# Moving a stack's load behind the shift rows on the SP queue, and splitting the wait ahead of them

## Chip, core and metric

The kernel runs on one core of one Trainium2 chip. The metric is the device time of one execution in microseconds. Engines are named as in the profile: PE (TensorE matmul), PEld (its weight loads), DVE (VectorE), ACT (ScalarE), POOL (GpSimd) and SP (SyncE, which computes nothing here and issues nearly all DMAs).

## What is computed

One transformer layer in float32 on x of shape 2 x 1024 x 512: `x = x + attn(layernorm(x))`, then `x = x + ffn(layernorm(x))`. The diff touches the attention:

```python
qkv = clip(einsum('bsd,ed->bse', x, Wqkv), -8, 8); q, k, v = split(qkv)
q = layer_norm(q, q_ln_w, q_ln_b); k = layer_norm(k, k_ln_w, k_ln_b)   # then 32 heads of 16
scores = einsum('bqhd,bkhd->bhqk', q, k) * 0.25 + slope[h] * (key - query)
probs = softmax(where(key <= query, scores, -1e30))
out = einsum('bsd,ed->bse', einsum('bhqk,bkhd->bqhd', probs, v), Wout)
```

The feed-forward part is a 512 x 512 matrix that is summed from four sign matrices with their row factors.

## The kernel before, in words

**Three stages.** First 16 tiles of 128 rows are normalised, projected, and q and k are split into three bf16 parts each (high, middle, low), turned and stored to DRAM in `parts_dram`; v goes to `v_dram`. Then 16 groups of heads (GROUPS; a group is 4 heads of one of the two sequences) go through the attention. Last, 16 output tiles take the output projection and the feed-forward part.

**A group.** Its scores are products of bf16 stacks. The *first* stack (`first_q`, `first_k`) has the three leading products of parts and six bias rows, the *second* (`second_q`, `second_k`) the three smaller products, rows for the causal steps, and two rows with the *shift*: the negative of each query's maximum over its keys, as a high and a low bf16 part. Each is held in a ring of three buffers (STACKS = 3). For each group PE first makes the scores of the first stack alone (`score_max`, L1078), and DVE takes their maxima (`take_max`, L951). DVE joins them (L921), PE turns them (L1147), ACT negates them and writes `shift` and `shift_hi` (L764, L765; each counts up `shift_hi_ready`), and POOL makes `shift_lo` (L653, which counts up `shift_ready`). SP copies the four rows (high and low, for two halves of the partitions) into `second_q` (`load_shift`, L476), each row 4 KB. Only then can the group's own scores be made with both stacks (`score`, L1098), which ACT exponentiates (L781) and PE multiplies by v (`weigh`, L1133). After each half of the queries ACT copies the sums out (`copy_half`, L809) and SP stores them.

**The order on PE, DVE, ACT and POOL** is written out by steps: a group has 40 of them (NE = 40 entries), and step s of each engine's `exp_step` does entry s of the exponentials and, beside it, one piece of the maxima of a later group. With EARLY = 14, the maxima of group k+2 begin at step 26 of group k, and the maxima of group k+1 are turned at step 28 of group k (TURN_AT = 28), so 12 steps are left until group k+1 begins at step 40. At a group's first step PE waits for `second_loaded` and `shift_loaded` (L1092, L1093). Before the first piece of the maxima it waits for `first_loaded` (L1066).

**The order on SP** is the order of `group_step(s)`, one call per group, and SP works through it strictly in turn: a wait on SP holds back everything behind it. Before: for group s+2, wait until group s-1's scores are done (L495), `load_first` (16 DMAs: twelve of 64 KB from `parts_dram`, L428, and four bias rows, L436) and `load_second` (14 DMAs: twelve of 64 KB and two bias rows; for groups 0 to 2 also four with step rows, L449); then `load_values(s+1)` (L468, 512 KB), behind a wait for the last product with v of group s-1; then the stores of the second half of group s-1 and the first half of group s (L506, 256 KB each), behind the waits for their copies; then `load_shift(s+1)`, behind its wait (L472). Groups 0 and 1 have their stacks loaded during the projections, and `load_shift(0)` stands ahead of the first call of `group_step`.

Of the kernel before, what the change touches and what calls it, by code (L numbers as in the profile page):

```python
# [24 lines left out]
GROUPS = BATCH * HEADS // G  # L25
# [152 lines left out]
def build(nc, x, wqkv_t, qk_w, qk_b, wout_t, bases_t, alphas, bias_rows, step_rows, masks, out):  # L178
# [7 lines left out]
    def sem(name):  # L186
        return ctx.enter_context(nc.semaphore(name))
# [8 lines left out]
    with ctx:  # L196
# [121 lines left out]
        shift_hi_ready, shift_ready = sem("shift_hi_ready"), sem("shift_ready")  # L318
# [54 lines left out]
        def _(sp):  # L373
# [48 lines left out]
            def load_terms(n, i, dst, terms, loaded):  # L422

                for half in range(PAIR):
                    for r, term in enumerate(terms):
                        at = half * HALF_ROWS + r * HD
                        slot = term[0] if i == 0 else 5 - term[1]
                        sp.dma_start(dst[at:at + HD, :, :],  # L428
                                     parts_dram[slot, n // GPB, n % GPB * HD:(n % GPB + 1) * HD, half]
                                     ).then_inc(loaded, 16)  # L430

            def load_bias(n, i, dst, row, last, loaded):

                for half in range(PAIR):
                    at = half * HALF_ROWS + NT * HD
                    sp.dma_start(dst[at:at + last - row, :, :], bias_rows[i, n % GPB, half, row:last]).then_inc(loaded, 16)  # L436

            def load_first(n):
                for i, dst in ((0, first_q[n % STACKS]), (1, first_k[n % STACKS])):
                    load_terms(n, i, dst, TERMS[:NT], first_loaded[n % STACKS])  # L440
                    load_bias(n, i, dst, 0, BIAS_ROWS, first_loaded[n % STACKS])

            def load_second(n):
                loaded = second_loaded[n % STACKS]
                for i, dst in ((0, second_q[n % STACKS]), (1, second_k[n % STACKS])):
                    if n < STACKS:
                        for half in range(PAIR):
                            at = half * HALF_ROWS + SECOND_K
                            sp.dma_start(dst[at:at + STEP_ROWS, :, :], step_rows[i]).then_inc(loaded, 16)  # L449
                    load_terms(n, i, dst, TERMS[NT:], loaded)  # L450
                load_bias(n, 1, second_k[n % STACKS], BIAS_ROWS, BIAS_ROWS + SHIFT_ROWS, loaded)
# [15 lines left out]
            def load_values(n):  # L467
                sp.dma_start(v_sb[n % 2][:], v_dram.rearrange("b g k p n -> (b g) k p n")[n]  # L468
                             .rearrange("k p n -> p k n")).then_inc(v_loaded[n % 2], 16)

            def load_shift(n):
                sp.wait_ge(shift_ready, n + 1)  # L472
                for r, part in ((0, shift_hi), (1, shift_lo)):
                    for half in range(PAIR):
                        row = half * HALF_ROWS + NT * HD + r
                        sp.dma_start(second_q[n % STACKS][row:row + 1, :, :].rearrange("p a t -> p (a t)"),  # L476
                                     part[n % 2][half * PAIR * TPB:(half + 1) * PAIR * TPB, :]
                                     ).then_inc(shift_loaded[n % 2], 16)
# [6 lines left out]
            projections_over()  # L485
            load_last_weights()
            load_shift(0)
            parts_over()

            def group_step(s):  # L490

                n = s + 2
                if 2 <= n < GROUPS:
                    if n >= STACKS:
                        sp.wait_ge(scored, NE * (n - STACKS + 1))  # L495
                    load_first(n)
                    load_second(n)

                n = s + 1
                if 2 <= n < GROUPS:  # L500
                    sp.wait_ge(pv_done, NU * (n - 1))
                    load_values(n)
                for n, half in ((s - 1, 1), (s, 0)):
                    if 0 <= n < GROUPS:
                        sp.wait_ge(o_ready, 2 * n + half + 1)
                        sp.dma_start(o_dram[n // GPB, :, ds((n % GPB) * G, G), half * BANK:(half + 1) * BANK]  # L506
                                     .rearrange("r j t -> j r t"), o_sb[half][:]).then_inc(o_stored[half], 16)

                n = s + 1
                if 1 <= n < GROUPS:  # L510
                    load_shift(n)

                if s == GROUPS - 2:
                    load_sums(0)
                if s == GROUPS - 1:
                    store_inverses(0)

                    sp.wait_ge(inv_stored, 16)
                    sp.wait_ge(wout_ready, DC)
                    sp.wait_ge(wffn_ready, DC)  # L520
                    for t in range(3):
                        if t == 2:
                            sp.wait_ge(att_ready, 1)
                        load_sums_of_tile(t)
                        load_residual(t)

            def load_sums_of_tile(t):

                sp.dma_start(o_in[t % 2][:], o_dram[t // TPB, 0:HD, :, ds((t % TPB) * P, P)]
                             .rearrange("(c r) h t -> (r h) c t", c=DC)).then_inc(o_loaded[t % 2], 16)  # L530
                rows = inv_dram[t // TPB, :, ds((t % TPB) * P, P)]
                sp.dma_start(inv_in[t % 2][:], rows.rearrange("(a h) t -> a h t", a=1)
                             .broadcast_to([HD // DC, HEADS, P])).then_inc(o_loaded[t % 2], 16)

            def load_residual(t):
                sp.dma_start(x2[t % 4][:], x[t]).then_inc(xr_loaded[t % 4], 16)

            def load_sums(b):

                for half in range(2):  # L540
                    sp.wait_ge(o_stored[half], 16 * (GROUPS if b else GROUPS - 1 - half))
                sp.dma_start(sums[:, b, :], o_dram[b, HD].rearrange("h (q t) -> (h q) t", q=P // HEADS)
                             ).then_inc(sums_loaded, 16)

            def store_inverses(b):
                sp.wait_ge(inverted, b + 1)
                sp.dma_start(inv_dram[b].rearrange("h (q t) -> (h q) t", q=P // HEADS),
                             inv[:, b, :]).then_inc(inv_stored, 16)

            run_groups(sp, group_step)  # L550

            def output_step(s):
# [722 lines left out]
```

## Time and profile before

| | us |
|---|---|
| median of 3 runs | 721.72 |
| lowest and highest of them | 720.21 and 725.4 |
| the profiled execution's own time | 724.78 |
| its span, first to last instruction | 723.0 |

The span is what the rows below are taken from; 1.8 us of the profiled execution lie outside it. Times of rows are microseconds from the start of the span. A "releaser" is what ended the idle time before an instruction, as inferred from semaphores; "issue" means that the profile shows no releaser. SPq is SP's queue of DMA issues: the duration there is what SP spent on issuing, not the transfer. "To landing" is from the issue to the last byte.

### The profile page before, as it was taken

To read this page: it belongs to the slowest core of one execution; us is meant where nothing else is said; L and a number is where in the kernel's file an instruction comes from. 1 tells how busy PE (TensorE), PEld (TensorE's weight loads), DVE (VectorE), ACT (ScalarE), POOL (GpSimd) and SP (SyncE) were. 2 spreads that over 40 slices of the span, in tenths; PEclk is the share of its full clock that TensorE was granted. 3 is DMA by queue.
4 is the path that set the end of the run, shared out by engine and by line. 5 is a ranking of instruction groups with operands and counts; after the bars stand their busy time and mean duration, and the time that the engine had idled before them with its cause. 6 is when DMAs were issued, how large, how long until landed. Compare 5 with 4: busy or idle time off the path is not lost.

```text
span 723.0 us, 16007 instructions
## 1 busy us (share of the span) xinstructions
PE 678.8 (94%) x6096; PEld 416.4 (58%) x6096; DVE 575.2 (80%) x990; ACT 411.4 (57%) x855; POOL 312.9 (43%) x403
## 2 busy tenths in 40 slices
PE   3999999997999999999999999999899896599998
PEld 2888888883354454444455455444445532488886
DVE  6799999988999889998998899799899810275664
ACT  5132333232078778887787788678778886222221
POOL 1377777777034625525426422322332234444440
PEclk9999999997579999999999999999999999699999
DMA  8225556777884342343344334324434111635441
GB/s 297 65 68 174 175 175 194 199 201 215 264 183 106 117 127 86 98 125 116 90 123 122 91 108 125 110 78 125 114 94 117 50 35 23 170 103 156 145 148 66
DMA packets 102060, 93.64 MB, mean 130 GB/s; under 512 B 11640, under 2 KB 81912, under 8 KB 101984
## 3 DMA queue, kind: packets, MB, share of 16 engines
q1 hardware_dynamic: 97856, 86.84, 41.4%
q10 hardware_dynamic: 2016, 3.67, 1.7%
q0 software_dynamic: 2112, 2.10, 1.5%
q8 instruction: 49, 0.80, 0.5%
q14 instruction: 27, 0.22, 0.1%
HBM read 57.44 MB, written 33.82 MB: 126 GB/s over the span
## 4 chain that ended last, share of the span: by engine, by line
PE 71%; DVE 15%; issue 8%; POOL 3%; ACT 2%; DMA 1%; SPq 0%; DVEq 0%; POOLq 0%; ACTq 0%
PE ps L1098 23%; PE ps L1133 20%; PE ps L1078 9%; PE ps L1012 5%; PE ps L1013 5%; PE ps L1014 5%; DVE stats L951 3%; DVE qk_stat L896 2%; DVE qk L892 2%; PE ps L1020 2%; PE ps L1074 2%; DVE x_stat L862 1%; DVE xt_lo L855 1%; DVE rest L871 1%; DVE v_ext L905 1%
## 5 line engine op out<-in xcount | busy, mean ns | idle before, releaser
L951 DVE TENSOR_REDUCE stats<-ps 128x1 f32<-128x512 f32 (+3 forms) x608 | 359.4, 656 | 43.9 <-PE ps L1078 42.2
L781 ACT ACTIVATE probs<-ps 128x512 f32<-128x512 f32 (+2 forms) x640 | 310.2, 560 | 83.4 <-PE ps L1098 82.9
L1078 PE MATMUL ps<-first_k,first_q 54*128 54x128 bf16 (+3 forms) x1152 | 219.9, 284 | 5.6 <-DVE stats L951 5.2
L1098 PE MATMUL ps<-second_q,second_k 64*128 64x128 bf16 (+4 forms) x1152 | 206.2, 276 | 0.0
L1098 PE MATMUL ps<-first_q,first_k 54*128 54x512 bf16 (+3 forms) x768 | 197.0, 331 | 9.3 <-issue 9.2
L673 POOL TENSOR_SCALAR_AFFINE_SELECT probs<-probs 128x256 f32<-128x256 f32 x256 | 102.5, 406 | 144.2 <-ACT probs L781 136.9
L1133 PE MATMUL ps<-probs,v_sb 128*32 128x512 f32 (+3 forms) x1536 | 157.9, 498 | 1.8 <-issue 0.8
L1098 PEld LDWEIGHTS ps<-first_q,first_k 54*128 54x128 bf16 x768 | 58.2, 95 | 121.8 <-ACT probs L781 108.1
L1078 PEld LDWEIGHTS ps<-first_k,first_q 54*128 54x128 bf16 x1152 | 92.7, 96 | 49.3 <-DVE stats L951 34.7
L1098 PEld LDWEIGHTS ps<-second_q,second_k 50*128 50x128 bf16 (+1 forms) x1152 | 92.9, 96 | 21.4 <-issue 2.1
L1012 PE MATMUL ps<-wqkv_hi,xt_hi 128*128 128x512 f32 x192 | 77.3, 403 | 0.0
L1014 PE MATMUL ps<-wqkv_hi,xt_lo 128*128 128x512 f32 x192 | 75.8, 395 | 0.0
L1013 PE MATMUL ps<-wqkv_lo,xt_hi 128*128 128x512 f32 x192 | 75.7, 394 | 0.0
L614 POOL TENSOR_TENSOR qk<-qk,qk_gain 128x1024 f32<-128x1024 f32 x16 | 38.4, 2399 | 59.9 <-DVE qk L913 59.9
L653 POOL TENSOR_TENSOR shift_lo<-shift,shift_hi 32x128 bf16<-32x128 f32 x16 | 6.7, 418 | 131.8 <-ACT shift_hi L765 131.8
L973 DVE TENSOR_TENSOR x<-ps,x 128x512 f32<-128x512 f32 x16 | 11.0, 687 | 58.9 <-PE ps L1014 58.9
L1133 PEld LDWEIGHTS ps<-probs,v_sb 128*32 128x32 f32 x1536 | 33.9, 108 | 34.9 <-ACT probs L781 15.1
L1074 PE MATMUL ps<-mask_sb 64*128 64x256 bf16 x256 | 51.0, 280 | 0.0
L751 ACT ACTIVATE qk_sd<-qk_mv,eps 128x2 f32<-128x2 f32 x16 | 4.7, 296 | 69.6 <-DVE qk_mv L899 69.6
L1014 PEld LDWEIGHTS ps<-wqkv_hi,xt_lo 128*128 128x128 f32 x192 | 36.6, 191 | 8.0
L1012 PEld LDWEIGHTS ps<-wqkv_hi,xt_hi 128*128 128x128 f32 x192 | 36.8, 191 | 7.2
L1013 PEld LDWEIGHTS ps<-wqkv_lo,xt_hi 128*128 128x128 f32 x192 | 36.7, 191 | 7.2
(79 smaller groups left out, 822.1 us busy)
## 6 DMA issues: line engine op xcount, KB each, us to landing
parts_dram<-parts SPq DMA_DIRECT2D x48, 256.0 KB, 4.0
v_dram<-v_ext SPq DMA_DIRECT2D x16, 512.0 KB, 4.0
v_sb<-v_dram SPq DMA_DIRECT2D x16, 512.0 KB, 4.4
o_dram<-o_sb SPq DMA_DIRECT2D x32, 256.0 KB
first_q<-parts_dram SPq DMA_DIRECT2D x96, 64.0 KB
first_k<-parts_dram SPq DMA_DIRECT2D x96, 64.0 KB
second_q<-parts_dram SPq DMA_DIRECT2D x96, 64.0 KB
second_k<-parts_dram SPq DMA_DIRECT2D x96, 64.0 KB
```

The lines of the kernel that those rows point to most:

```text
L614: pool.tensor_tensor(qk[t % 2][:], qk[t % 2][:], qk_gain[:], ALU.mult).then_inc(qk_scaled, 1)
L673: pool.affine_select(out=turned, in_=turned, compare_op=ALU.is_ge, fill=0.0, base=0, pattern=[[0, 2], [1, P]], channel_multiplier=-1).then ...
L781: act.activation(weights, scores, ACT.Exp, scale=SCALE).then_inc(exp_done, 1)
L892: dve.tensor_scalar(qk[t % 2][:], ps[:, bank:bank + 2, :], CLIP, -CLIP, ALU.min, ALU.max).then_inc(qk_clipped, 1)
L951: dve.tensor_reduce(to, scores, AX.X, ALU.max).then_inc(max_taken, 1)
L1012: pe.matmul(to, hi[:, c, :], w_hi[:, c, :], start=(c == 0), stop=False)
L1013: pe.matmul(to, hi[:, c, :], w_lo[:, c, :], start=False, stop=False)
L1014: last = pe.matmul(to, lo[:, c, :], w_hi[:, c, :], start=False, stop=(c == DC - 1))
L1074: pe.matmul(ps[:, bank, :].rearrange("p (r h t) -> p r h t", r=G, h=2)[:, :, h, :], late_q[h][mine, :], one_hot[mine, :, :], start=(h == 0 ...
L1078: last = pe.matmul(ps[:, bank, r * cols:(r + 1) * cols], first_q[n % STACKS][rows, hp, i * P:(i + 1) * P], first_k[n % STACKS][rows, hp, k ...
L1098: return pe.matmul(ps[:, bank, r * cols + first:r * cols + last], stack_k[n % STACKS][rows, heads[r] // PAIR, kb * P:(kb + 1) * P], stack_ ...
L1133: last = pe.matmul(ps[j * VW:(j + 1) * VW, PV_BANK, to:to + cols], v_sb[n % 2][:, kb, j * VW:(j + 1) * VW], probs[w % P_SLOTS][:, j, 0:col ...
```

## The change

In `load_shift(n)` SP issues the two high rows after `shift_hi_ready` has reached 2(n+1), which both copies of ACT give, and waits for `shift_ready` only ahead of the two low rows. In `group_step` `load_second(s+2)` no longer stands behind `load_first(s+2)`, but behind `load_shift(s+1)`.

```diff
             def load_shift(n):
-                sp.wait_ge(shift_ready, n + 1)
                 for r, part in ((0, shift_hi), (1, shift_lo)):
+                    if r == 0:
+                        sp.wait_ge(shift_hi_ready, 2 * (n + 1))
+                    else:
+                        sp.wait_ge(shift_ready, n + 1)
                     for half in range(PAIR):
                         row = half * HALF_ROWS + NT * HD + r
                         sp.dma_start(second_q[n % STACKS][row:row + 1, :, :].rearrange("p a t -> p (a t)"),
...
                     if n >= STACKS:
                         sp.wait_ge(scored, NE * (n - STACKS + 1))
                     load_first(n)
-                    load_second(n)
...
                 n = s + 1
                 if 1 <= n < GROUPS:
                     load_shift(n)
+
+                n = s + 2
+                if 2 <= n < GROUPS:
+                    load_second(n)
```

## Rows read from the trace of the kernel before

**Rows 1.** The page's busy times: us (share of the span) xinstructions

```profile
PE 678.8 (94%) x6096; PEld 416.4 (58%) x6096; DVE 575.2 (80%) x990; ACT 411.4 (57%) x855; POOL 312.9 (43%) x403
```

**Rows 2.** Waits, PE's: us in total, times, longest us

```profile
PE ps L1098 <- issue: 9.2, 7, 1.9
...
PE ps L1133 <- ACT o_sb L809: 0.7, 2, 0.4
```

**Rows 3.** Timeline of PE, short stretches: start us, us, instruction [idle before <-releaser]

```profile
243.31 0.28 PE L1147 MATMUL ps<-ident,peak 128*32 128x128 f32 x1
...
296.21 0.28 PE L1147 MATMUL ps<-ident,peak 128*32 128x128 f32 x1
...
321.03 0.28 PE L1147 MATMUL ps<-ident,peak 128*32 128x128 f32 x1
...
330.35 0.37 PE L1098 MATMUL ps<-first_q,first_k 54*128 54x512 bf16 x1 [1.69 <-issue]
...
347.72 0.28 PE L1147 MATMUL ps<-ident,peak 128*32 128x128 f32 x1
...
579.94 0.27 PE L1147 MATMUL ps<-ident,peak 128*32 128x128 f32 x1
```

**Rows 4.** Timeline of SP's queue, groups 4 and 5

```profile
319.84 1.19 SPq L506 DMA_DIRECT2D o_dram<-o_sb  x2
322.83 2.23 SPq L476 DMA_DIRECT2D second_q<-shift_hi  x2
325.10 1.23 SPq L476 DMA_DIRECT2D second_q<-shift_lo  x2
328.69 2.64 SPq L428 DMA_DIRECT2D first_q<-parts_dram  x6
...
342.44 1.19 SPq L506 DMA_DIRECT2D o_dram<-o_sb  x2
349.51 1.20 SPq L476 DMA_DIRECT2D second_q<-shift_hi  x2
```

**Rows 5.** Tile shift_lo's transfers, windows 322:331, 349:354 and 195:200.6 in turn

```profile
DMA to landing us min/median/max: 4.0/4.3/4.5
...
DMA to landing us min/median/max: 2.1/2.2/2.2
...
DMA to landing us min/median/max: 1.8/1.8/1.8
```

**Rows 6.** Waits of SP's DMA queue: us in total, times, longest us

```profile
SPq L476 <- POOL shift_lo L653: 66.9, 16, 6.9
...
SPq L428 <- PE ps L1098: 40.4, 13, 3.7
```

**Rows 7.** Windows: us, PE, PEld, DVE, ACT, POOL busy, PEclk, DMA share, GB/s

```profile
252.00:257.00 5.00, 4.34 (x36) 1.97 (x40) 3.06 (x5) 2.59 (x5) 0.77 (x3) 0.69 0.38 112
...
252.70:278.70 26.00, 25.89 (x304) 12.96 (x306) 22.26 (x38) 19.87 (x42) 7.16 (x16) 0.93 0.36 104
...
457.70:483.80 26.10, 25.97 (x303) 12.98 (x304) 22.25 (x38) 19.86 (x42) 5.91 (x15) 0.93 0.35 102
```

**Rows 8.** Timeline of SP's queue at the start of the attention

```profile
198.88 2.84 SPq L428 DMA_DIRECT2D first_q<-parts_dram  x6
...
205.84 0.74 SPq L449 DMA_DIRECT2D second_q<-in_step_rows  x2
...
214.08 0.58 SPq L436 DMA_DIRECT2D second_k<-in_bias_rows  x2
```

**Rows 9.** Timeline of ACT and of POOL at the turn in group 4

```profile
322.05 0.26 ACT L765 ACTIVATE shift_hi<-ps 32x128 bf16<-32x128 f32 x1
...
322.38 0.42 POOL L653 TENSOR_TENSOR shift_lo<-shift,shift_hi 32x128 bf16<-32x128 f32 x1 [9.37 <-ACT shift_hi L765]
```

**Rows 10.** Timeline of ACT and of DVE in group 5

```profile
342.23 0.59 ACT L809 ACTIVATE o_sb<-ps 128x512 f32<-128x512 f32 x1
...
347.18 0.25 DVE L921 TENSOR_REDUCE peak<-stats 128x32 f32<-128x96 f32 x1
```

## The prediction

> **What bounds the kernel now.** I read the page's busy times first, then the waits, then the timeline around them. PE is busy for 678.8 us, 94% of the span, and no other engine comes over 80% [rows 1], so only PE's idle time can be won, and what a stall costs it beside that. The change touches SP alone, in the attention. There the waits of PE are few: seven times it stood ahead of a product of L1098 with no releaser shown, 9.2 us in all and up to 1.9 [rows 2]. One of the seven is the row at 330.35, idle 1.69 us before it [rows 3], and it is the first product of group 5. Two semaphores are waited for there, the second stack's and the shift rows'. The stack was issued a whole group earlier. The shift rows were not: SP issued the two low ones from 325.10 for 1.23 us [rows 4], the last of them thus at about 325.7, and the longest landing of the two is 4.5 us [rows 5], which gives 330.2. So the shift rows end this wait. SP itself has time: it waits 66.9 us for shift_lo in 16 waits, and 40.4 us for PE at the head of a group's step [rows 6].
>
> What the stalls cost can be read without adding up gaps. Every group turns its maxima at the same step. From 296.21 to 321.03 no stall lies between, and the distance is 24.82 us; from 321.03 to 347.72, across the stall at 330.35, it is 26.69 [rows 3]. So this stall of 1.69 costs 1.87, as PE has to fill its buffers again. From the turn at 243.31 to the one at 579.94 there are 13 groups in 336.63 us, where 13 x 24.82 are 322.66: 14.0 us too many [rows 3]. They hold all seven stalls, and something else too: two groups, from 252.70 and from 457.70, took 26.0 and 26.1 us without a stall at their end, and the mean granted clock in both is 0.93; in the first of them it is 0.69 from 252.0 to 257.0 [rows 7], so the lower of the two levels (1.2 instead of 2.4 GHz) was granted early in the group. Against 24.82 this cost 1.2 and 1.3 us. Both groups began with a stall; yet that at 330.35 brought no dip, as its 26.69 is 24.82 and the 1.87 above. So 14.0 is about 9.2 of idle time, 2.5 of clock, 1.3 of refilling (seven times 0.18) and 0.7 of waits for o_sb in the last groups [rows 2], which the change leaves, with 0.3 over.
>
> **Why the rows land late.** Three cases stand in [rows 4, 5]. Ahead of group 5 the stores of o_sb are issued until 321.03 and the high rows from 322.83, 1.8 us later: the low rows take 4.0 to 4.5 us to land. Ahead of group 6 the stores end at 343.63, the high rows start at 349.51, 5.9 us later: 2.1 to 2.2 us. At the start of the attention, with nothing before them for a long time and a load issued right behind them (198.88) [rows 8], they take 1.8 us. So what is issued shortly before the rows holds them up, and what is issued behind them does not. What stands before them is a burst: 30 loads of stacks in about 13 us, 512 KB of v, and two stores of 256 KB.
>
> **The change, part by part.** *The split wait.* Now the high rows wait for POOL's shift_lo, which takes 0.42 us and ends at 322.80; ACT's copy ends at 322.31 [rows 9]. After it the high rows start 0.5 us sooner. A pair takes about 1.2 us to issue [rows 4], more than those 0.5, so the low rows find their wait over and also go 0.5 us sooner, not 1.2. The wait added on shift_hi_ready costs nothing: what stands behind it on SP stood behind a later wait before. Alone this part is worth 0.5 us of each stall.
>
> *The moved load.* Take group 5 (starts 330.35) as the pattern, times from its start. Before, first and second stack go out in one run, then v, then the stores until +13.3 (343.63), and the high rows at +19.2. After, only the first stack is issued early in the step, six terms in 2.64 us [rows 4] and two bias rows in 0.58 [rows 8], both twice, with small gaps: 6.6 us. The store of the first half must wait for its copy, which ends at 342.82 [rows 10], +12.5; the store, one of 0.6 us, is out at +13.1. The v load and the other store, which had stood right before it, go 3 us earlier, at about +10. The high rows start at +18.6, 5.5 us behind a store of 256 KB that is alone, nearly what gave 2.1 to 2.2 us. In a group like 4, where the old run ended 1.8 us ahead of the rows, 6 us of issuing are gone from before them. So the last low row is issued at 18.6 + 1.9 = +20.5 and lands at +22.7. The next group starts at +24.7. This leaves 2.0 us, more than one long issue costs (1.0: two high rows took 2.23 in one case and 1.20 in the other) [rows 4]. Value: the stalls vanish, and with them the clock's two dips, 14.0 - 0.7 = 13.3 us. Bounds: 14.0 if all goes; from below 7 x 0.5 = 3.5 if the landings stay as late as they are.
>
> *The second stack, where it goes now.* Its 14 issues start at +21.1 and take two times 2.64 and 0.58 [rows 4, 8] with small gaps, 6.0 us, until +27.1; it is needed a group and a half later, so it costs nothing itself. But SP's queue is past the next group's start (+24.7) by 2.4 us, and by 3.4 with one long issue. The wait at L428, which hid behind 40.4 us of idling, gets shorter and pays for it. The first stack of the next step is then issued from +2.4 to +9.0. PE wants it where DVE joins the maxima before, 347.18 [rows 10], +16.8. So 7.8 us are left for landing and long issues; the longest landing of a row shown is 4.5 us. Costed at nothing, in all groups but one. In group 1 the stack moved behind the rows is group 2's, with step rows: at the start of the attention it took from 205.84 to 214.66, 8.8 us [rows 8]. Group 1 starts at about 243.31 - 17.37 = 225.9 (its turn, less what lies from start to turn in group 5) [rows 3]. By the pattern the moved stack goes out 3.6 us before that, at 222.3, and ends at 231.1; the first stack ends at 237.7, or 238.7 with one long issue, and is wanted at 225.9 + 16.8 = 242.7. That leaves 4.0 to 5.0 us for a landing which for the rows was 1.8 to 4.5 and may be longer for a load behind 18 others (6 us as my upper estimate, the 4.5 and a third more): a wait of 0 to 2.0. I take 0.7, and 0.3 for shift rows that this makes late once, 1.0 in all.
>
> **The sum.** 724.8 - 13.3 + 1.0 = 712.5 for an execution like the profiled one. The median is 3.1 us lower, and the three runs spread over 5.2 us. Stalls and dips are what can differ from run to run, as the long issues and the dips come where they like; a kernel without them should be steadier, but part of the 3.1 may lie elsewhere. I take off half: 711.0, 10.7 us or 1.5% below the median. A measurement here can tell about 1% from no change.
>
> The Trainium skill (DMA: Bandwidth & Descriptors, section "Anatomy of one DMA — SWDGE (gpsimd) path") fits a DMA as about 2.0 us fixed plus its bytes over the bandwidth, given for POOL's path. For a row of 4 KB that is 2.0 us whatever stands before it. By it the last row ahead of group 5 would have landed at 327.7, and the stall would be another's. Those landings [rows 5] agree with it for the quiet cases (1.8 and 2.2) and not for 4.0 to 4.5. The case in which it holds is the third rival.
>
> **Rivals.**
> 1. *The rows stay late.* If the one store ahead of them holds them up as two stores and a v load did, only the 0.5 us come off: 7 x 0.5 = 3.5, so 721.72 - 3.5 = 718.2. For it: the store writes to DRAM and is the last thing before the rows in both orders. Against it: 5.9 us after two of them nothing was left.
> 2. *The clock dips anyway.* PE stands idle no more, yet the two dips stay: 711.0 + 2.5 = 713.5. For it: a stall of 1.69 us had none, so the stall alone doesn't decide. Against it: both came early in a group that a stall had opened.
> 3. *Not the load.* The rows land late for a cause that isn't in SP's order, and the 0.5 us is eaten by it: 721.7, no change.
> 4. *The first stack becomes late, slower.* Place: PE's wait for first_loaded in each group from 1 to 12. It decides from the point where the first stack takes over 7.8 us from its last issue to landing, as it now queues behind 14 loads issued right before it, and no longer into an empty queue. At 9.1 us it costs 1.3 us in each of 12 groups, 15.6, and keeps the dips (2.5): 711.0 + 18.1 = 729, which is slower than before. For it: a backlog of 30 loads plainly is there now, as it holds the rows up. Against it: these rows still land within 4.5 us with a v load and two stores on top.
>
> **Chances.** Forecast 0.62, rival 1 0.15, rival 2 0.12, rival 3 0.06, rival 4 0.05. The forecast's own range is from 707.7 (724.8 - 14.0 and the whole 3.1 off) to 714. The range given reaches to rival 1: 707.0 to 718.5. Faster by over 1% (below 714.5) is the forecast and most of rival 2: 0.72. Within 1%: rivals 1 and 3 and the rest, 0.24. Slower by over 1%: 0.04.
>
> **What would show it.** Right: the row "L1098 <- issue" of PE's waits falls from 9.2 us in seven to under 2; shift_lo's landings have a longest of under 3 us; SP's order shows second_q behind shift_lo; turn to turn is 24.8 us in nearly all groups and their clock 1.00. The wait of SP at L428 falls well below 40.4 us. Wrong: PE's waits at L1098 stay near half of what they were (rival 1), or a new wait of PE ahead of L1078 with no releaser shows, near 16.8 us into a group (rival 4), or groups without a stall keep a clock of 0.93 (rival 2).

## The result, and the profile after

| | before, us | after, us |
|---|---|---|
| median (6 runs each) | 724.71 | 711.43 |
| lowest and highest | 720.21 to 727.1 | 709.58 to 712.45 |
| the profiled execution | 724.78 | 710.61 |
| its span | 723.0 | 708.9 |

The ratio on record is 0.983, 95% interval 0.980 to 0.986: 1.7% faster (the two medians alone give 0.982). The forecast was 711.0 in a range of 707.0 to 718.5, so the time is right. The gain against these six runs, 13.3 us, is more than the 10.7 forecast from three of them; on the chips of the experiments the kernel before has medians of 720.67 to 722.53, and in run 10 the changed kernel is 11.8 us ahead of it. The runs also lie closer together, 2.9 us apart against 6.9. The changed kernel's lines have moved: L1098 of before is L1104, L1078 is L1084, L1147 is L1153, L951 is L957, the stores' L506 is L508 and the rows' L476 is L479.

The page of the changed kernel has for all products of the scores with the first stack, those at the groups' starts among them (busy us, mean ns | idle us before them):

```profile
L1104 PE MATMUL ps<-first_q,first_k 54*128 54x512 bf16 (+3 forms) x768 | 193.8, 328 | 0.1
```

The idle time before them is 0.1 us, where the waits had 9.2 in seven [rows 2]. The turns in PE's timeline, as in [rows 3]:

```profile
241.91 0.28 PE L1153 MATMUL ps<-ident,peak 128*32 128x128 f32 x1
...
316.35 0.28 PE L1153 MATMUL ps<-ident,peak 128*32 128x128 f32 x1
...
341.17 0.28 PE L1153 MATMUL ps<-ident,peak 128*32 128x128 f32 x1
...
565.26 0.27 PE L1153 MATMUL ps<-ident,peak 128*32 128x128 f32 x1
```

From 316.35 to 341.17 are 24.82 us, and from 241.91 to 565.26, the same 13 groups, 323.35. That is 0.7 us over 13 x 24.82, where it was 14.0. Of the span's 14.2 us, 13.3 are gained here; 1.4 more were gained ahead of the first of these turns (nearly all of it in the projections, where the two kernels don't differ) and 0.5 lost behind the last. The windows of two groups, columns as in [rows 7], show a granted clock of 1.00 where it was 0.93:

```profile
249.30:274.10 24.80, 24.80 (x311) 12.39 (x308) 22.66 (x39) 20.25 (x44) 8.08 (x19) 1.00 0.37 109
447.80:472.60 24.80, 24.80 (x311) 12.39 (x308) 22.67 (x39) 20.25 (x44) 6.84 (x18) 1.00 0.42 116
```

SP's timeline around group 5, which starts at 323.71, answers to [rows 4]:

```profile
326.78 0.58 SPq L436 DMA_DIRECT2D second_k<-in_bias_rows  x2
327.40 2.62 SPq L428 DMA_DIRECT2D first_q<-parts_dram  x6
...
334.28 0.67 SPq L436 DMA_DIRECT2D first_k<-in_bias_rows  x2
335.00 0.39 SPq L468 DMA_DIRECT2D v_sb<-v_dram  x1
335.43 1.42 SPq L508 DMA_DIRECT2D o_dram<-o_sb  x2
342.46 1.20 SPq L479 DMA_DIRECT2D second_q<-shift_hi  x2
343.71 1.21 SPq L479 DMA_DIRECT2D second_q<-shift_lo  x2
```

The lines show that the moved stack ends at 327.36, inside the next group, and the first stack at 334.95, +11.2. The stores end at 336.85, +13.1, and the rows follow 5.6 us later. (Where the text says that a store ends, its issue is meant; it lands later.) All low rows of the kernel, before and after in turn:

```profile
DMA to landing us min/median/max: 1.7/2.5/5.0
```

```profile
DMA to landing us min/median/max: 1.7/1.8/3.5
```

The longest landing of after, 3.5 us, is ahead of group 12 and cost nothing, as 0.67 us were left. Its row was issued 7.5 us behind the stores, and those had landed before; what held it isn't known.

What SP pays is in its waits; the second row was 40.4 us [rows 6]:

```profile
SPq L508 <- ACT o_sb L815: 37.4, 16, 8.3
...
SPq L428 <- PE ps L1104: 0.7, 3, 0.3
```

### The profile page after: what moved, and what is told of

Its sections match the earlier page's. It is cut to its first block, busy times and chain, and to the rows that moved or that the text cites. A ratio compares the mean times of both kernels' runs of the same rounds, so it can differ in the third digit from the quotient of the medians.

```text
span 708.9 us, 16007 instructions
## 1 busy us (share of the span) xinstructions
PE 674.5 (95%) x6096; PEld 413.3 (58%) x6096; DVE 575.5 (81%) x990; ACT 410.3 (58%) x855; POOL 313.2 (44%) x403
## 4 chain that ended last, share of the span: by engine, by line
PE 73%; DVE 15%; issue 7%; POOL 2%; DMA 2%; ACT 1%; SPq 0%; DVEq 0%; POOLq 0%; ACTq 0%
PE ps L1104 23%; PE ps L1139 20%; PE ps L1084 9%; PE ps L1018 6%; PE ps L1020 5%; PE ps L1019 5%; DVE stats L957 4%; PE ps L1026 2%; DVE qk_stat L902 2%; DVE qk L898 2%; PE ps L1080 2%; DVE x_stat L868 1%; DVE xt_lo L861 1%; DVE rest L877 1%; DVE v_ext L911 1%
## 5 line engine op out<-in xcount | busy, mean ns | idle before, releaser
L957 DVE TENSOR_REDUCE stats<-ps 128x1 f32<-128x512 f32 (+3 forms) x608 | 358.3, 656 | 31.6 <-PE ps L1084 29.3
L1084 PE MATMUL ps<-first_k,first_q 54*128 54x128 bf16 (+3 forms) x1152 | 217.3, 282 | 5.1 <-DVE stats L957 4.5
L1104 PE MATMUL ps<-second_q,second_k 64*128 64x128 bf16 (+4 forms) x1152 | 204.6, 273 | 0.0
L1104 PE MATMUL ps<-first_q,first_k 54*128 54x512 bf16 (+3 forms) x768 | 193.8, 328 | 0.1
L1104 PEld LDWEIGHTS ps<-first_q,first_k 54*128 54x128 bf16 x768 | 57.6, 94 | 110.5 <-ACT probs L787 107.6
L1084 PEld LDWEIGHTS ps<-first_k,first_q 54*128 54x128 bf16 x1152 | 92.3, 96 | 51.0 <-DVE stats L957 36.0
L1104 PEld LDWEIGHTS ps<-second_q,second_k 50*128 50x128 bf16 (+1 forms) x1152 | 91.7, 95 | 21.0 <-issue 0.6
```

Source lines behind the costliest of these rows:

```text
L957: dve.tensor_reduce(to, scores, AX.X, ALU.max).then_inc(max_taken, 1)
L1084: last = pe.matmul(ps[:, bank, r * cols:(r + 1) * cols], first_q[n % STACKS][rows, hp, i * P:(i + 1) * P], first_k[n % STACKS][rows, hp, k ...
L1104: return pe.matmul(ps[:, bank, r * cols + first:r * cols + last], stack_k[n % STACKS][rows, heads[r] // PAIR, kb * P:(kb + 1) * P], stack_ ...
```

## The experiments

All times are medians. Ratios are against the kernel before on the same chip, with their 95% interval.

**1. The split wait alone.** The kernel before, with only this:

```diff
             def load_shift(n):
-                sp.wait_ge(shift_ready, n + 1)
                 for r, part in ((0, shift_hi), (1, shift_lo)):
+                    if r == 0:
+                        sp.wait_ge(shift_hi_ready, 2 * (n + 1))
+                    else:
+                        sp.wait_ge(shift_ready, n + 1)
```

> The kernel before with the split wait alone; the load stays where it was. Theory (the rows land late because of the loads and stores issued shortly before them; the split gives only the 0.5 us by which ACT's copy is earlier than POOL's): stalls stay at 5 to 7 groups, each shorter by up to 0.5 us, so 2 to 4 us faster than before (before: 724.7 median of six), with 0 to 2 dips of the clock left; the low rows' landings still reach 4 to 5 us. Rival (the split carries the gain, since the low rows leave 1.2 us sooner): stalls nearly gone, 9 us faster or more, about 713.

Measured: 722.70, ratio 1.0017 (0.9985 to 1.0049): nothing, at most 0.2% of gain. The waits of PE in its profile, SP's stores and the high rows ahead of group 5, their low rows' landings, and the stall:

```profile
PE ps L1101 <- issue: 6.8, 6, 2.3
```

```profile
317.25 1.19 SPq L509 DMA_DIRECT2D o_dram<-o_sb  x2
320.01 1.52 SPq L479 DMA_DIRECT2D second_q<-shift_hi  x2
```

```profile
DMA to landing us min/median/max: 4.3/4.6/4.8
```

```profile
327.62 0.37 PE L1101 MATMUL ps<-first_q,first_k 54*128 54x512 bf16 x1 [1.28 <-issue]
```

The stores ended at 318.44, and PE could go on at 327.62, 9.2 us later. Before, the stores ended at 321.03 and PE went on at 330.35 [rows 3, 4], 9.3 us later. The high rows left 1.3 us behind the turn's start at 318.71 instead of 1.8, and the low ones took longer to land, 4.3 to 4.8 us against 4.0 to 4.5 [rows 5]. So it isn't their issue that sets when they land, but when the stores went out. Both theories fall: the split gives neither 9 us nor 0.5 us a stall.

**2. The moved load alone.** The changed kernel with the old wait:

```diff
                 for r, part in ((0, shift_hi), (1, shift_lo)):
-                    if r == 0:
-                        sp.wait_ge(shift_hi_ready, 2 * (n + 1))
-                    else:
-                        sp.wait_ge(shift_ready, n + 1)
```

(and `sp.wait_ge(shift_ready, n + 1)` ahead of the loop again).

> The changed kernel with the old single wait on shift_ready; the load stands behind the rows. Theory: in the changed kernel the last row landed 0.67 us or more before each group's first product, 2.4 us in the typical group, so 0.5 us later rows still arrive in time: no stall or one of 0.1, turns 24.8 us apart, the time within 0.3% of the changed kernel's 711.4, landings 1.8 to 3.5 us. Rival (the split is needed too): stalls in several groups, 714 or more.

Measured: 711.29, ratio 0.9861 (0.9828 to 0.9894), turns 24.8 us apart in the profiled execution, from the second to the fifteenth. One of the six runs took 715.53, the others 708.81 to 711.89; it wasn't profiled, so stalls can't be ruled out there. The theory holds: the move is all of the gain that can be measured, and the split shows none in either order.

**3. The second stack right ahead of the rows.** The changed kernel with these two in the other order:

```diff
+                n = s + 2
+                if 2 <= n < GROUPS:
+                    load_second(n)
+
                 n = s + 1
                 if 1 <= n < GROUPS:
                     load_shift(n)
-
-                n = s + 2
-                if 2 <= n < GROUPS:
-                    load_second(n)
```

> The changed kernel, but the second stack goes out after the stores and right ahead of the rows' wait, so it is out of the first stack's run and yet ahead of the rows: 14 loads from +13.1 to +19.1 of a group, the rows from +19.2. Theory (what is issued shortly before the rows holds them up): a stall in every group, landings of 3 to 5 us, 1 to 2.5 us each, 15 to 35 us slower than the changed kernel, so slower than before. Rival A (only the stores to DRAM hold the rows up, loads into the chip's memory don't): rows land in about 2 us, no more than 0.6 us late in issue, no stalls, about 711 to 714. Rival B (it is the length of the run of 30 loads that matters): no stalls either.

Measured: 713.48, ratio 0.9892 (0.9861 to 0.9923). SP's timeline ahead of the rows for group 6, those low rows' landings, and PE's waits:

```profile
339.32 3.32 SPq L428 DMA_DIRECT2D second_q<-parts_dram  x6
342.69 3.98 SPq L428 DMA_DIRECT2D second_k<-parts_dram  x6
346.71 0.57 SPq L436 DMA_DIRECT2D second_k<-in_bias_rows  x2
347.32 1.20 SPq L479 DMA_DIRECT2D second_q<-shift_hi  x2
```

```profile
DMA to landing us min/median/max: 1.8/1.8/1.8
```

```profile
PE ps L1104 <- issue: 0.9, 1, 0.9
```

My theory expected a stall in every group here. With 14 loads issued up to the last 0.04 us before them, the rows land in 1.8 us, as fast as anywhere. The rows were issued late instead (3.7 us behind the turn at 343.58, where 1.3 is usual), which cost one stall, in group 1. The last low rows ahead of groups 1 to 15 took 1.8 us in 12 cases; the others are 2.1, 2.6 and 3.3 us, with the stores issued 8 us and more before. So 14 such loads hold the rows up little or not at all.

**4. The store behind the rows.** The kernel before, the second stack in its old place, with

```diff
-                for n, half in ((s - 1, 1), (s, 0)):
+                for n, half in ((s - 1, 1),):
...
                     load_shift(n)
+                for n, half in ((s, 0),):
+                    if 0 <= n < GROUPS:
+                        sp.wait_ge(o_ready, 2 * n + half + 1)
+                        sp.dma_start(o_dram[...], o_sb[half][:]).then_inc(o_stored[half], 16)
```

> The kernel before with the store of the first half's sums moved behind the rows; the load stays. Ahead of the rows stand then the 30 loads, v and one store that is issued 0.6 us sooner. Theory (the whole backlog counts, of which this store is one of 32 transfers): stalls shrink a little, 1 to 5 us faster than before, landings still up to 3 to 4.5 us. Rival (the store to DRAM, being the last thing ahead of the rows, is what they wait for): landings of about 2 us, stalls gone, about 711.

Measured: 710.53, ratio 0.985 (0.982 to 0.988), no stall. One store out of the way gives all that the change gives, with all 30 stack loads in their old place. This is the rival that I had written down against my own theory. The rows still don't all land in 1.8 us: the last low row takes up to 3.2, with v and one store ahead of it.

**5. v behind the rows.** The kernel before, both stores ahead of the rows:

```diff
-                n = s + 1
-                if 2 <= n < GROUPS:
-                    sp.wait_ge(pv_done, NU * (n - 1))
-                    load_values(n)
...
                     load_shift(n)
+                n = s + 1
+                if 2 <= n < GROUPS:
+                    sp.wait_ge(pv_done, NU * (n - 1))
+                    load_values(n)
```

> The kernel before with the 512 KB load of v moved behind the rows; the 30 stack loads and both stores stay ahead of them. What the runs so far left: the last row lands no earlier than 9.0 to 10.1 us after the last store's issue in the kernel before, 7 us with one store less. Theory S (the two stores to DRAM hold the rows): nothing changes but 0.4 us of SP's issuing, the last row still lands 8.5 us or more after the stores' issue, stalls in 4 to 7 groups, 717 or more. Theory B (the burst of v and two stores, 1 MB issued in 1.6 us, drains at some 120 GB/s whatever it is): half of it is gone, the last row can land 5 us after the stores, no stalls, about 711.

Measured: 713.09, ratio 0.990 (0.985 to 0.994), with two stalls, 0.8 us in all. Theory S had expected four to seven and theory B none.

**6. A load in the store's place.** As 4, and where the store had been:

```diff
+                if 0 <= s < GROUPS:
+                    sp.wait_ge(o_ready, 2 * s + 1)
+                    if s:
+                        sp.wait_ge(spare_loaded, 16 * s)
+                    sp.dma_start(spare[:], x[0]).then_inc(spare_loaded, 16)
```

> As the run with the first half's store behind the rows, but in the store's old place, behind the same wait, a load of 256 KB (128 rows of 2 KB, one tile of x into a spare tile) is issued: the same bytes in the same place, read into the chip's memory instead of written to DRAM. This load is extra work that the kernel doesn't need. Theory S (only stores to DRAM hold the rows): landings stay at 1.8 to 3.2 us, no stalls, about 711. Theory B (bytes): landings of 3 to 5 us where the load is issued within 3 us of the rows, stalls in 4 to 7 groups, 717 or more.

Measured: 711.97, ratio 0.987 (0.982 to 0.992). The three and the kernel before are best compared ahead of one group, the 14th, where the last of these transfers was issued shortly before the rows. SP's timeline of the kernel before, then of 4, 5 and 6, each with the landings of its low rows:

```profile
550.77 0.39 SPq L468 DMA_DIRECT2D v_sb<-v_dram  x1
551.20 1.19 SPq L506 DMA_DIRECT2D o_dram<-o_sb  x2
...
556.37 1.22 SPq L476 DMA_DIRECT2D second_q<-shift_lo  x2
```

```profile
DMA to landing us min/median/max: 3.3/4.0/4.7
```

```profile
538.38 0.39 SPq L468 DMA_DIRECT2D v_sb<-v_dram  x1
538.81 0.58 SPq L506 DMA_DIRECT2D o_dram<-o_sb  x1
...
543.17 1.21 SPq L476 DMA_DIRECT2D second_q<-shift_lo  x2
```

```profile
DMA to landing us min/median/max: 2.4/2.4/2.5
```

```profile
539.75 1.19 SPq L502 DMA_DIRECT2D o_dram<-o_sb  x2
...
545.21 1.22 SPq L476 DMA_DIRECT2D second_q<-shift_lo  x2
```

```profile
DMA to landing us min/median/max: 2.5/2.9/3.4
```

```profile
540.20 0.39 SPq L470 DMA_DIRECT2D v_sb<-v_dram  x1
540.63 0.59 SPq L508 DMA_DIRECT2D o_dram<-o_sb  x1
541.32 0.41 SPq L515 DMA_DIRECT2D spare<-in_x  x1
...
544.50 1.22 SPq L478 DMA_DIRECT2D second_q<-shift_lo  x2
```

```profile
DMA to landing us min/median/max: 2.4/3.3/4.3
```

The last low row starts halfway through its pair, so its landing is that time plus the longest. From the start of the burst's first issue to this landing, ahead of this group and ahead of groups 2 to 14 in each trace:

| what goes out ahead of the rows, within 1.6 us (2.5 at most) | ahead of group 14, us | over the groups, us |
|---|---|---|
| v and two stores (before) | 557.0 + 4.7 - 550.8 = 10.9 | 10.4 to 12.0, 13.1 once |
| two stores (5) | 545.8 + 3.4 - 539.8 = 9.4 | 9.4 to 10.2 |
| v, one store, one load of the store's size (6) | 545.1 + 4.3 - 540.2 = 9.2 | 9.2 to 10.1 |
| v and one store (4) | 543.8 + 2.5 - 538.4 = 7.9 | 7.9 to 9.3 |

(Longer ones stand where the rows went out late enough to land in their 1.8 us.) By group 14 v's 512 KB are worth 1.5 us, a load of 256 KB 1.3, and this store of the same 256 KB 3.0; that is one group of one trace each. Neither theory holds alone: the burst counts as such (B), but the store counts for about twice a load of its size (S). The waits at the groups' first products order themselves alike: 9.2 us before, 0.8 in 5, 0.9 in 6, none in 4.

That it goes to DRAM is not what makes this store dear. The first line is of stores to DRAM of the same size, at the end of the kernel before (KB each, median us from issue to landing), the second the load of 6:

```profile
out<-y_out SPq DMA_DIRECT2D x16, 256.0 KB, 2.1
```

```profile
spare<-in_x SPq DMA_DIRECT2D x16, 256.0 KB, 7.4
```

Two stretches of the kernel before, columns as in [rows 7], in each of which a single one of these stores was going: one of `o_sb`, issued at 575.34, and the last of `y_out`, issued at 720.54.

```profile
576.50:580.50 4.00, 3.99 (x48) 2.17 (x45) 2.74 (x5) 2.88 (x7) 0.00 (x0) 1.00 0.24 62
```

```profile
721.00:722.00 1.00, 0.00 (x0) 0.00 (x0) 0.00 (x0) 0.00 (x0) 0.00 (x0) 1.00 0.63 240
```

So 256 KB can go to DRAM in 2 us, at up to 240 GB/s, and a store of `o_sb`, alone, goes at 62 GB/s with a quarter of the 16 DMA engines busy (0.24). The trace's packets agree: four are in flight at once for most of the first stretch, 16 or 17 for most of the second. Each store of `o_sb` also raises its semaphore in four steps behind its issue; the stores of `y_out`, the load of 6 and the rows do it in 16. I read this as a store that runs on four engines; its destination is laid out with the group's four heads outermost (L506).

By its last step a store of `o_sb` has landed 5.8 us after its issue when alone, and 8.3 to 10.0 us as the second of two in groups 2 to 14. The last low row then lands 0.7 to 1.0 us behind the last step of the last store, in each of these groups of the kernel before but the two in which the rows went out late. In 6 the load of 256 KB itself takes 7.4 us, with v and one such store ahead of it, and the row lands 0.7 to 1.3 us behind it. So what counts is when the last large transfer is done, and the stores of `o_sb` are slow as they seem to use few engines. The experiment for it, the same store spread over all 16, was not run.

**7. The rows on another queue.** The kernel before, where ACT issues the four rows on its own queue behind its copies:

```diff
             def load_shift(n):
-                sp.wait_ge(shift_ready, n + 1)
...
+                pass
...
                     act.activation(shift_hi[n % 2][:], turned, ...).then_inc(shift_hi_ready, 1)
+                    act.wait_ge(shift_hi_ready, 2 * (n + 1))
+                    load_rows(act, n, 0, shift_hi)
+                    act.wait_ge(shift_ready, n + 1)
+                    load_rows(act, n, 1, shift_lo)
```

> The kernel before with the four rows issued by ACT instead of SP, on ACT's own queue; ACT waits for shift_lo itself. All of SP's order stays, less the rows. Theory Q (the rows wait in SP's queue for what stands ahead): on another queue they land 1.7 to 2.3 us after their issue in every group, no stall at the groups' first products; what ACT loses by issuing, some 2.5 us a group, may show as other waits. Theory E (the completion of a row waits at the DMA engine for earlier writes of other queues as well, as a rule of the Trainium skill's page DMA: Bandwidth & Descriptors, section Queues, rings and completion order, has it): landings still reach 3.5 us or more where the stores stand shortly before, and stalls stay.

Measured: 756.58, ratio 1.049 (1.042 to 1.057), as ACT stands still for some 3 us a group. SP's stores and ACT's rows ahead of group 5, then the low rows' landings of that group and of group 1, whose rows go out 6.1 us behind the last store:

```profile
329.31 1.08 SPq L507 DMA_DIRECT2D o_dram<-o_sb  x2
```

```profile
331.52 1.15 ACTq L375 DMA_DIRECT2D second_q<-shift_hi  x2
332.71 1.81 ACTq L375 DMA_DIRECT2D second_q<-shift_lo  x2
334.62 1.57 ACT L786 ACTIVATE probs<-ps 128x512 f32<-128x512 f32 x3 [3.14 <-issue]
```

```profile
DMA to landing us min/median/max: 4.0/4.6/5.2
...
DMA to landing us min/median/max: 1.8/1.8/1.8
```

(`load_rows` issues the two rows that had stood in the loop of `load_shift`.) The rows are as late on ACT's queue as on SP's. So they don't stand in line in SP's queue alone; they are held where both queues meet. This is what the Trainium skill has (DMA: Bandwidth & Descriptors, section "Queues, rings and completion order"): both queues run on the same engines, and the write that counts up a semaphore lands only after every earlier write of its DMA engine, of other queues too. The run agrees with it, as the rows of groups 2 to 14 are complete from 0.7 us behind the last store's last step to 0.2 us ahead of it. It doesn't tell this order of writes from plain sharing of the engines' time.

**8. The first stack issued later.** The changed kernel, with the store of 4 out of the rows' way and 14 more loads of 64 KB into spare tiles behind the moved stack:

```diff
                     load_second(n)
+                    if n > 2:
+                        sp.wait_ge(spare_loaded, 16 * 14 * (n - 2))
+                    for k in range(14):
+                        at = k % 8 * 16
+                        sp.dma_start(spare[k // 8][at:at + HD, :, :], ...).then_inc(spare_loaded, 16)
```

> The changed kernel with 14 further loads of 64 KB (into spare tiles, extra work) behind the moved second stack, and with the first half's store behind the rows so that it can't hold them up. It tries the prediction's fourth rival: the first stack's issue ends at +15.3 of a group instead of +9.0 and is wanted at +16.8. If the first stack lands 2 us after its last issue: PE waits 0.5 us ahead of L1078 in each of about 12 groups, 713 to 720. If it lands at once with the queue (loads don't pile up) but long issues of 1 to 2 us fall into the run: waits of 1 to 2.5 us in half the groups, 718 to 728. If no wait shows, the slack of the first stack was larger than the prediction had it.

Measured: 768.74, ratio 1.066 (1.059 to 1.074). PE's waits, and SP's last loads of group 5's first stack with PE's first product of it:

```profile
PE ps L1099 <- DMA first_k<-in_bias_rows: 32.7, 12, 6.8
```

```profile
303.14 0.65 SPq L438 DMA_DIRECT2D first_k<-in_bias_rows  x2
```

```profile
305.36 0.61 PE L1099 MATMUL ps<-first_k,first_q 54*128 54x512 bf16 x1 [3.80 <-DMA first_k<-in_bias_rows]
```

The prediction's fourth rival exists, and is dearer than I expected: 32.7 us of waits in 12 groups, and with refilling and dips of the clock 48 us too many between the turns. The stack landed 1.6 us after SP was done with issuing it, so the queue holds it up little; it is SP's issuing that was late. PE wanted it at 305.36 - 3.80 = 301.56, 17.1 us into the group (started at 284.47), so its issue has to end by +15.5. In the changed kernel it ends between +10.3 and +12.8.

**9 to 11. On one chip.** The changed kernel with the store of 4 as well, the changed kernel again, and kernel 4 again. The edit of the first, against the changed kernel:

```diff
-                for n, half in ((s - 1, 1), (s, 0)):
+                for n, half in ((s - 1, 1),):
...
                     load_shift(n)
+                for n, half in ((s, 0),):
...
                     load_second(n)
```

> The changed kernel with the first half's store behind the rows and ahead of the moved second stack. In the changed kernel PE's turns are 24.81 us apart everywhere and the rows have 0.67 us or more to spare. Theory (PE's own work is the bound now): more slack for the rows (2.4 us in nearly every group), the same time as the changed kernel within 0.3%, 710 to 712. Rival (other executions than the profiled one still have stalls, which this removes): 1 to 2 us below the changed kernel.

> The changed kernel itself, beside the other two on one chip: 711 within 1 us, no stalls at L1104.

> The kernel before with the first half's store behind the rows alone, again, beside the changed kernel on one chip: the same as the changed kernel within 0.3% by the theory that both have no stalls left; if the 0.9 us between their medians on two chips was real, 710.5 against 711.4 again.

Measured: 711.09, 710.74 and 710.89, ratios 0.9841, 0.9831 and 0.9835, each with an interval of 0.004 to either side. All three have turns 24.8 us apart and 0.7 to 0.8 us too many over 13 groups. No difference shows between them: the 0.9 us by which 4 had seemed ahead did not come again, and none of the versions beats the change. In this stage PE's own work is the bound: in the two windows of the changed kernel above it is busy for 24.80 of 24.80 us.

## Why the prediction was right, and where it was not

*What bounds the kernel, and what is to be won:* right. The seven stalls, the refilling and the two dips of the clock were 13.3 us by the turns, and 13.3 us it was.

*The moved load, the times:* right to 0.4 us at the end of the chain. The stores' end was forecast at +13.1 and is at +13.1; the high rows at +18.6 and are at +18.8; the gap 5.5 and is 5.6; 2.0 us to spare, and 2.4 were left where no long issue came. Wrong on the way: v and the second half's store were to go at about +10, 3 us earlier, and leave the last store alone. They went at +11.3 and +11.7, 0.4 us earlier than before, and the two stores still stand together.

*Why the rows land late:* wrong in its cause. The prediction said that "what is issued shortly before the rows holds them up" and named the burst of "30 loads of stacks in about 13 us, 512 KB of v, and two stores of 256 KB" as one. Runs 3 and 4 take it apart. The stack loads count for little or nothing as a backlog: SP needs 0.42 us to issue each of those of 64 KB, and right behind 14 of them a row landed in 1.8 us (run 3). What counts are the large transfers in the last 1.6 us or so of the burst, and the two stores most, which seem to run on a quarter of the engines. In the seven groups with a stall the last row landed 9.0 to 10.1 us after the last store's issue, however early it was issued itself. The loads matter by keeping SP busy: the first half's sums are ready at +12.5 of a group, but before, SP was done with storing them between +13.3 and +17.7, as its long issues fell. With 24.8 us to the next group, the limit is between +14.7 and +15.8, and the groups bear it out: the six larger stalls stand behind the six groups at +16.2 and more, the smallest (0.23 us) behind one at +15.0, none behind one at +15.5. The change brings the end of that store to +13.1 in group 5, 11.7 us ahead of the start. So the move helps as forecast because it lets a store go sooner, and not because it takes loads away. That the forecast of the stalls came true is in part luck: its cause, fewer loads ahead of the rows, and the true one, an earlier store, come with the same edit.

*The split wait:* mis-sized. "Alone this part is worth 0.5 us of each stall" came out as nothing (run 1), since the landing hangs on the stores. With it the lower bound of 3.5 us and rival 1's price were wrong: had the rows stayed late, the gain would have been 0. *Rival 1* fell in its time, but its suspicion was the right one: it named the store as the last thing before the rows.

*The second stack, where it goes now:* right that it costs nothing. The wait at L428 went from 40.4 to 0.7 us. The first stack's issue was forecast to end at +9.0 and ends at +10.3 to +12.8: the moved stack ends at +3.7 instead of +2.4 in group 5, and long issues are more frequent than the one allowed for. So of the 7.8 us of slack only 4.3 to 6.8 were left (17.1 less those), which was enough, as the landing took 1.6 us in run 8 and not the 4.5 allowed for. The 1.0 us for group 1 did not come: its first stack ended at +12.8, later than the +11.8 forecast, and still landed in time. *Rival 4* is real only in run 8, where 14 more loads were added.

*The sum:* 712.5 for the profiled execution against 710.6. The difference is this 1.0 and the 0.9 us outside the attention. The 1.5 us taken off for the median was luck. Its reason holds in part, as the runs are steadier now, but the changed kernel's median is 0.8 us above its profiled execution and not below; the 1.5 just cover most of the 1.9 that the sum missed.

*The signs:* four of the five for "right" came; the landings' longest was to be under 3 us and is 3.5. *Rival 2* fell: no dip is left in the attention. *Rival 3* fell as well: the cause was in SP's order, though not in the loads. The Trainium skill's fit of about 2.0 us fixed (DMA: Bandwidth & Descriptors, section "Anatomy of one DMA — SWDGE (gpsimd) path") agrees roughly with the landings now, with a median of 1.8 us; it doesn't with what stores ahead make of them.

## What to carry to other kernels

A small transfer whose landing is on the path is held up by large ones issued shortly before it, and it didn't help here to issue it a little sooner or from another engine; put the large ones behind it, or well ahead. Look at how long each large one takes and how many DMA engines it keeps busy, not at its bytes or direction alone: the worst here was a store on what looks like four of 16. Spreading it wider may do as much as moving it, but that wasn't tried. Loads that a queue can only issue slowly, like the stacks' here, didn't pile up, but they keep the queue from a store that is ready, so look at what stands behind a long run of issues as well as at the run. And where two causes lie together in time, as loads and stores here, a forecast can be right for the wrong one: move each alone.

## What the runs showed of the hardware that I had not expected

- Two stores of 256 KB to DRAM, each going alone, took 5.8 us (`o_sb`, at 62 GB/s) and 2.0 us (`y_out`, at up to 240 GB/s) in the kernel before.
- A store of `o_sb` put off the landing of a small transfer behind it by about 3.0 us, a load of 256 KB by 1.3 (group 14 in the kernel before, in 6 and in 4). The row landed 0.7 to 1.3 us behind the last of them.
- Fourteen loads (twelve of 64 KB, two of 8 KB) right ahead of a row of 4 KB left its landing at 1.8 us (run 3, group 6).
- A row on ACT's queue waited for SP's stores as one on SP's did, 4.0 to 5.2 us ahead of group 5.
- A dip of the clock follows a stall of PE, but not by its length alone: before, stalls of 1.71 and 1.68 us had one, and stalls of 1.69 and 1.91 had none; in run 1 one of 2.28 had one, and one of 1.28 had none; in run 8 one of only 1.21, at 448.23, was followed by one (granted clock 0.51 from 449.9 to 453.4).
